# Row maxima split before they are turned: identity products in place of transposes, and a shorter VectorE list

## What is computed

```python
x = x + jnp.tanh(g_xattn[0]) * _L0_xattn_ref(_layernorm(x, axis=-1), ctx_1024, ...)
x = x + jnp.tanh(g_ffn[0]) * _L0_ffn_ref(_layernorm(x, axis=-1), ...)
# ... the same for layers 1, 2 and 3, each with its own attention and its own FFN
```

```python
attn = jnp.einsum('bhnd,bhmd->bhnm', q * scaling, k)
attn = jax.nn.softmax(attn, axis=-1)
out = jnp.einsum('bhnm,bhmd->bhnd', attn, v)
```

## Time and profile before

| | us |
|---|---|
| median of 3 runs | 1301.12 |
| lowest and highest of the 3 | 1295.35 and 1309.11 |
| span of the profiled execution | 1295.3 |
| TensorE busy in that span | 978.6 (76%) |
| VectorE busy | 778.0 (60%) |
| ScalarE busy | 570.7 (44%) |
| GpSimd busy | 391.1 (30%) |

### The profile page before, as it was taken

One profiled execution on the slowest core, in us unless ns is written; L12 is line 12 of the kernel. 1 busy time (PEld: TensorE's weight loads), 2 busy tenths in 40 slices (PEclk: granted clock), 3 DMA queues, 4 the chain that ended last, 5 costly groups with the idle time before them and its releaser, 6 DMA issues. The chain is left out here.

```text
span 1295.3 us, 19254 instructions
## 1 busy us (share of the span) xinstructions
PE 978.6 (76%) x5366; PEld 728.4 (56%) x5366; DVE 778.0 (60%) x1924; ACT 570.7 (44%) x1101; POOL 391.1 (30%) x519
## 2 busy tenths in 40 slices
PE   3788475688888988488888889478867578883765
PEld 2566353565565655256666666356755347773554
DVE  3687565576676667356666656447665424444665
ACT  1566242365455555245555554246643233321553
POOL 2432002122223213235555556423310132210212
PEclk9899576777677668689999999779987789996878
DMA  4000000000000000000000000100000100000001
GB/s 116 1 1 1 1 1 19 1 18 17 18 17 17 11 5 17 1 0 1 1 1 0 0 1 1 35 1 1 1 18 1 50 15 1 0 0 1 1 0 33
DMA packets 25577, 13.74 MB, mean 11 GB/s; under 512 B 10775, under 2 KB 25006, under 8 KB 25390
## 3 DMA queue, kind: packets, MB, share of 16 engines
q1 hardware_dynamic: 25518, 13.03, 3.7%
HBM read 11.98 MB, written 1.05 MB: 10 GB/s over the span
## 5 line engine op out<-in xcount | busy, mean ns | idle before, releaser
L1473 POOL TENSOR_TENSOR L1f_h<-L1f_h,L1f_gb 128x512 f32<-128x512 f32 (+1 forms) x96 | 151.6, 1581 | 120.0 <-DVE L1f_h L1763 99.5
L719 ACT ACTIVATE L_pt<-bank 128x512 f32<-128x512 f32 x224 | 131.0, 597 | 62.7 <-PE bank L605 59.6
L706 ACT ACTIVATE L_part<-bank,L_bias_ca,const 128x256 fp32r<-128x256 f32 x128 | 68.7, 562 | 118.7 <-PE bank L546 118.7
L407 POOL TENSOR_TENSOR L_kc<-L_kc_all,const 128x256 fp32r<-128x256 f32 x96 | 58.8, 616 | 186.3 <-PE bank L605 130.8
L1763 DVE TENSOR_TENSOR L1f_h<-L1f_a,bank 128x512 f32<-128x512 f32 (+1 forms) x96 | 65.5, 682 | 70.7 <-ACT L1f_a L1603 69.8
L1603 ACT ACTIVATE L1f_a<-bank 128x512 f32<-128x512 f32 (+1 forms) x96 | 57.2, 596 | 114.2 <-PE bank L1528 114.1
L1771 DVE TENSOR_TENSOR L1f_h_lo<-L1f_h,L1f_h_hi 128x512 fp32r<-128x512 f32 (+1 forms) x96 | 88.7, 925 | 11.3 <-ACT L1f_h_hi L1616 11.3
L845 DVE TENSOR_REDUCE L_ms<-bank 128x2 f32<-128x512 f32 x128 | 84.4, 687 | 16.1 <-PE bank L567 15.5
L567 PE MATMUL bank<-L_k,L_q 32*128 32x256 f32 x256 | 74.1, 402 | 11.9 <-DVE L_ms L845 8.9
L831 DVE SCALAR_TENSOR_TENSOR L_q<-bank,L_bias_c,L_part 128x256 fp32r<-128x256 f32 x96 | 46.3, 482 | 60.6 <-ACT L_part L706 56.0
L843 DVE TENSOR_REDUCE L_mc<-bank 128x8 f32<-128x512 f32 (+1 forms) x96 | 65.6, 683 | 22.8 <-PE bank L560 14.2
(11 more groups left out here) (405 smaller groups left out, 2613.4 us busy)
## 6 DMA issues: line engine op xcount, KB each, us to landing
L_raw<-in_L_ffn_w_dram SPq DMA_DIRECT2D x8, 176.0 KB, 2.3
L_raw<-in_L_ffn_v_dram SPq DMA_DIRECT2D x8, 176.0 KB, 2.4
const<-in_const_dram SPq DMA_DIRECT2D x1, 1036.0 KB, 4.9
x<-in_x_dram SPq DMA_DIRECT2D x2, 512.0 KB
L_raw<-in_L_ffn_w_dram SPq DMA_DIRECT2D x8, 128.0 KB, 2.4
L_mask<-in_mask_Bx1xSxS_ff_dram SPq DMA_DIRECT2D x2, 512.0 KB
out_dram<-x SPq DMA_DIRECT2D x2, 512.0 KB
L_raw<-in_L_ffn_w_dram SPq DMA_DIRECT2D x8, 48.0 KB, 2.5
```

The lines of the kernel that those rows point to most:

```text
L706: last = act.activation(part[:, i].bitcast(F32R), b_proj[:, i * S:(i + 1) * S], ACT.Identity, bias=bias_ca[:, i, g:g + 1], scale=pr.c("ak" ...
L719: act.activation(pt[:, g // 2, (g % 2) * NS + i], b_st[(g * NS + i) % 2][:], ACT.Exp, scale=scale).then_inc(sem["exp_done"], 1)
L1473: pool.tensor_tensor(h[0:m, r], h[0:m, r], gb[0:m, gate_slot(c)], ALU.mult).then_inc(sem["h_done"], 1)
```

## The change

Five edits, made in `attention` and, but for the second, in `attention3`.

1. VectorE no longer writes each maximum twice. It writes it once into the first row (`high`), and since `mx` is now fp32r the write rounds it. It then waits for its own write (`m_hi`) and writes what the rounding left into the second row (`low`). In layer 1 the maximum of `mc` and `ms` is also written whole into `m_all` beforehand, for that subtraction.
2. In layer 1 TensorE adds q into the same bank by a second product with the identity.
3. The two fp32 transposes of a group become ordinary products of fp32r operands with an fp32r copy of the identity, `ident_r`, which VectorE makes once in each layer's preparation.
4. ScalarE copies the bank into `mt` and raises `m_split` itself; it now waits until TensorE has used the older `mt`. The factors, `hm` and `hq` are gone.
5. VectorE's step `maxima` is gone, and with it the additions of 256 columns (L866, L868, L1247).

The core of the diff; `attention3` has the same edits but for `m_all` and q, and the rest are counts of the preparation and types.

```diff
-                        last = pe.transpose(b_mt[:, t * P:(t + 1) * P], mx[:, g % 2, t].rearrange("p j c -> p (j c)"), pr.id())
+                        ts = slice(t * P, (t + 1) * P)
+                        last = pe.matmul(b_mt[:, ts], mx[:, g % 2, t].rearrange("p j c -> p (j c)"), ident_r[:], start=True, stop=not gated)
+                        if gated:
+                            last = pe.matmul(b_mt[:, ts], ident_r[:], q[:, g, ts], start=False, stop=True)
                     last.then_inc(sem["m_turned"], 1)
...
                 def maxima(b, g):
                     act.wait_ge(sem["m_turned"], b * NG + g + 1)
-                    need(act, sem["m_split"], b * NG + g)
-                    act.activation(hm[:].bitcast(F32R), b_mt[:, 0:S], ACT.Copy, scale=pr.c("am1" if gated else "am")).then_inc(sem["m_hi"], 1)
+                    need(act, sem["st_done"], b * U + (g - 1) * NS)
+                    act.copy(mt[:, g % 2], b_mt[:, 0:S]).then_inc(sem["m_split"], 1)
...
+                prep(dve.tensor_copy(ident_r[:], pr.id()))
...
-                    dst = mx[:, g % 2].rearrange("p t j c -> p (t j) c")[:, :, at_row:at_row + 2]
-                    mcb = mc[:].rearrange("p t j -> p (t j)").unsqueeze(2).to_broadcast([P, 2 * GH, 2])
+                    high, low = (mx[:, g % 2, :, :, at_row + e] for e in range(2))
                     if own_keys:
-                        msb = ms[:].rearrange("p t j -> p (t j)").unsqueeze(2).to_broadcast([P, 2 * GH, 2])
-                        dve.tensor_tensor(dst, mcb, msb, ALU.max).then_inc(sem["m_ready"], 1)
+                        dve.tensor_tensor(m_all[:], mc[:], ms[:], ALU.max)
+                        dve.tensor_tensor(high, mc[:], ms[:], ALU.max).then_inc(sem["m_hi"], 1)
                     else:
-                        dve.tensor_copy(dst, mcb).then_inc(sem["m_ready"], 1)
-
-                def maxima(b, g):
+                        dve.tensor_copy(high, mc[:]).then_inc(sem["m_hi"], 1)
                     dve.wait_ge(sem["m_hi"], b * NG + g + 1)
-                    need(dve, sem["st_done"], b * U + (g - 1) * NS)
-                    if gated:
-
-                        need(dve, sem["m_split"], b * NG + g)
-                        dve.wait_ge(sem["qk_split"], b * NG + (g + 1))
-                        dve.tensor_tensor(hq[:], hm[:], q[:, g].bitcast(F32), ALU.add).then_inc(sem["hq_ready"], 1)
-                        dve.wait_ge(sem["hq_ready"], b * NG + (g + 1))
-                    dve.tensor_tensor(mt[:, g % 2], b_mt[:, 0:S], hq[:] if gated else hm[:], ALU.add).then_inc(sem["m_split"], 1)
+                    dve.tensor_tensor(low, m_all[:] if own_keys else mc[:], high.bitcast(F32), ALU.subtract).then_inc(sem["m_ready"], 1)
```

More of the change, by code:

```diff
@@ L209, in attention @@
         mc = sb("mc", [P, 2, GH])
-        mx = sb("mx", [P, 2, 2, GH, 32])
-        hm = sb("hm", [P, S])
+        mx = sb("mx", [P, 2, 2, GH, 32], F32R)
+        m_all = sb("m_all", [P, 2, GH])
+        ident_r = sb("ident_r", [P, P], F32R)
         mt = sb("mt", [P, 2, S], F32R)
@@ L251, in attention @@
         mask_a = sb("mask_a", [P, 1])
-        DVE_WEIGHTS = 10 if biased else 9
+        DVE_WEIGHTS = 11 if biased else 10
         DVE_READY = DVE_WEIGHTS + 4 + (2 if gated else 1) + (2 if masked else 0)
@@ L485, in _ @@
                 if biased:
-                    pe.wait_ge(sem["prep_dve"], 3)
+                    pe.wait_ge(sem["prep_dve"], 4)
                     for i in range(2):
@@ L903, in y @@
                     dve.scalar_tensor_tensor(xb, b_turn[:, 0:S].rearrange("p (t d) -> p t d", t=2), tg, xb, ALU.mult, ALU.add).then_inc(sem["x_done"], 1)
-                passes(dve, {"scale": scale_x, "turn": turn, "mask": mask, "proj": proj, "scores": scores, "maxima": maxima,
+                passes(dve, {"scale": scale_x, "turn": turn, "mask": mask, "proj": proj, "scores": scores,
                              "o_norm": o_norm, "o_scale": o_scale, "y": y})
@@ L940, in attention3 @@
         mc = sb("mc", [P, 2, H3])
-        mx = sb("mx", [P, 2, H3, 16])
-        hm = sb("hm", [P, S])
+        mx = sb("mx", [P, 2, H3, 16], F32R)
+        ident_r = sb("ident_r", [P, P], F32R)
         mt = sb("mt", [P, S], F32R)
@@ L1070, in _ @@
                 pe.wait_ge(sem["prep_act"], 12)
-                pe.wait_ge(sem["prep_dve"], 4)
+                pe.wait_ge(sem["prep_dve"], 5)
                 pe.wait_ge(sem["prep_pool"], 4)
@@ L1107, in maxima @@
                     for t in range(2):
-                        last = pe.transpose(b_mt[:, t * P:(t + 1) * P], mx[:, t].rearrange("p j c -> p (j c)"), pr.id())
+                        last = pe.matmul(b_mt[:, t * P:(t + 1) * P], mx[:, t].rearrange("p j c -> p (j c)"), ident_r[:], start=True, stop=True)
                     last.then_inc(sem["m_turned"], 1)
@@ L1184, in maxima @@
                     act.wait_ge(sem["m_turned"], b + 1)
-                    need(act, sem["m_split"], b)
-                    act.activation(hm[:].bitcast(F32R), b_mt[:, 0:S], ACT.Copy, scale=pr.c("a16")).then_inc(sem["m_hi"], 1)
+                    need(act, sem["st_done"], b * 2)
+                    act.copy(mt[:], b_mt[:, 0:S]).then_inc(sem["m_split"], 1)
                 def weights(b, h):
@@ L1216, in _ @@
                 dve.tensor_copy(self_[:].rearrange("p c n -> p (c n)"), pr.c("self3")).then_inc(sem["prep_dve"], 1)
+                dve.tensor_copy(ident_r[:], pr.id()).then_inc(sem["prep_dve"], 1)
                 dve.wait_ge(sem["prep_act"], 12)
@@ L1240, in scores @@
                     need(dve, sem["m_turned"], b)
-                    dve.tensor_copy(mx[:].rearrange("p t j c -> p (t j) c")[:, :, 0:2],
-                                    mc[:].rearrange("p t j -> p (t j)").unsqueeze(2).to_broadcast([P, 2 * H3, 2])).then_inc(sem["m_ready"], 1)
-                def maxima(b):
+                    dve.tensor_copy(mx[:, :, :, 0], mc[:]).then_inc(sem["m_hi"], 1)
                     dve.wait_ge(sem["m_hi"], b + 1)
-                    need(dve, sem["st_done"], b * 2)
-                    dve.tensor_tensor(mt[:], b_mt[:, 0:S], hm[:], ALU.add).then_inc(sem["m_split"], 1)
+                    dve.tensor_tensor(mx[:, :, :, 1], mc[:], mx[:, :, :, 0].bitcast(F32), ALU.subtract).then_inc(sem["m_ready"], 1)
                 def sums(b):
@@ L1270, in y @@
                     dve.scalar_tensor_tensor(xb, b_turn[:, 0:S].rearrange("p (t d) -> p t d", t=2), tg, xb, ALU.mult, ALU.add).then_inc(sem["x_done"], 1)
-                passes(dve, {"scale": scale_x, "turn": turn, "scores": scores, "maxima": maxima, "sums": sums, "parts": parts, "divide": divide, "y": y})
+                passes(dve, {"scale": scale_x, "turn": turn, "scores": scores, "sums": sums, "parts": parts, "divide": divide, "y": y})
 def ffn(pr, layer):
```

5 lines of the change are left out of this document (2 added, 3 removed).

## The result

| | before | after |
|---|---|---|
| median, us | 1300.79 | 1327.82 |
| lowest and highest | 1295.35, 1309.11 | 1317.45, 1329.29 |
| span of the profiled execution | 1295.3 | 1327.5 |

The ratio is 1.0177, with a 95% interval from 1.0122 to 1.0232: slower, by 27 us in the medians and 32 in the profiled executions. The forecast was 1323, with 1284 to 1338 as range. The number was met; most of its working was not, and the rest of this document is about that.

The account below looks back on a forecast made before the run. No engine is full: layers 0, 2 and 3 are rings of waits, layer 1 alternates between VectorE and TensorE. Layers 0 to 3 add +2.8, +12.5, +4 and +2.8, sum +22.1 us on 1295.3; against the median 1323, range 1284 to 1338.

Parts of the forecast that it names:

- cheap products: Rival on TensorE's new products: 0.11 us each, as fp32r or by the skill's table; total 1300, no change; chance 0.22.
- the new instruction has neither: TensorE: the product has neither transpose mode nor 256 columns, to which the low price belongs, so 0.22 us each.
- The lower bound of 0.10: TensorE: router logits with eight moving columns take 0.10 us each, so a full weight load is hardly cheaper than a transpose.
- dear products: Main case: each new TensorE product takes 0.22 us, +0.22 a group in layers 0, 2, 3, more in layer 1; chance 0.50.
- In the two at the lower clock TensorE pays 2 x 1.3: Layer 1: two of four groups a sequence run at the lower clock, each paying +1.3 us for four products.
- the clock in a rival: Rival on layer 1: relieved VectorE lets TensorE run without gaps, clock rises to 0.80, total 1286; chance 0.16.
- the hop: Layer 2: `m_split` comes from ScalarE, so some 0.55 of the mask's transposes' 0.67 us wait for L868 goes.
- 0 from the list: Layer 2: the gain from `m_split` is taken back, half by `low`, the rest by two other q writes; net 0.
- -0.8 on the list: Layer 0's q writes: two gain 0.1 us, one loses 0.2 to `low`, one gains 0.09; -0.1 a sequence.
- The place matters more: VectorE: `low` stands ahead of the q write, the wide addition stood behind it; `low` itself taken at 0.22 us.
- "collisions" rival: `m_all`, `high`, `low` stretched beside GpSimd, +0.39 us each: +12 in layer 1, some +4 elsewhere; total 1317; chance 0.12.
- VectorE's and ScalarE's terms: VectorE's small operations add 10 to 15 us busy time in layer 1; ScalarE's copy falls from 468 to 375 ns.

Follow-up runs that it names:

- the ninth experiment: Changed kernel with layer 1 put back as before the change, except that its two transposes are fp32r products; median 1326.45 us, ratio 1.0209 to the kernel before.
- The third experiment: Changed kernel with plain fp32 operands for the product that turns layer 1's maxima; median 1316.58 us, ratio 1.0104 to the kernel before.
- experiment 5: Changed kernel with layer 1 as before the change and `low` behind the q write in layers 0 and 2; median 1298.58 us, ratio 0.9923.
- 1: Changed kernel with layer 1 exactly as before the change; median 1302.22 us, ratio 1.0008 to the kernel before.
- 10: Changed kernel, but in layer 1 VectorE adds q and writes `mt`, and fp32 transposes turn the maxima; median 1297.6 us, ratio 0.9894 to the kernel before.
- 11: Layers 1 and 3 as before the change, layers 0 and 2 changed with `low` behind the q write; median 1291.49 us, ratio 0.9952.
- 12: Layer 1 of 10, layers 0 and 2 changed with `low` behind the q write, layer 3 as before the change; median 1288.8 us, ratio 0.9894.
- 2: Changed kernel, but in layer 1 VectorE adds q and writes `mt`, without TensorE's product with q; median 1316.75 us, ratio 1.0125 to the kernel before.

## Why the prediction was right, and where it was not

By its own last line the forecast was wrong in kind: it named two signs, cheap products and a clock of layer 1 that moves by over 0.05, and both came (0.05 us, and 0.60 for 0.71). That the number was met is luck.

**The price of the products: wrong.** The step was "the new instruction has neither, and is nearest to L661 in shape and four-byte operands. I take 0.22". It takes 0.05 at the upper clock as the second of a pair, and in layer 1's row of four up to 0.11 at the upper and 0.21 at the lower clock. The lower bound of 0.10 was wrong for a pair: I took it from the router logits, but those rows are plain fp32 records. For the row of four it came true. The chance of 0.50 rested on this one choice between two rows. By the Trainium skill's table ("VectorE: DVE Perf Modes", The TRN2 errata) a product of 128 columns takes, as an estimate, about 0.06 us. The pair's 0.05 agrees with it, the row of four doesn't, and I had set it aside with L661's 0.22, which only says that plain fp32 costs more.

**Layer 1, the number near, the mechanism missed.** I had +12.5 us from dear products at an unchanged clock (by its own terms, 1.6 x 8, it should read 12.8), and it was +29.5 us with cheap products at a lower clock. The step that failed is in the sum, "In the two at the lower clock TensorE pays 2 x 1.3": the number of groups at the lower clock was taken as given. I had the clock in a rival, but with the other sign: VectorE relieved, TensorE without gaps, clock up. What the runs showed in its place is that TensorE's own instruction in this spot carries the level: with products for transposes 80% of the time is at the lower level for 58%, and by the ninth experiment that alone costs 20 to 32 us. The third experiment has half of my dear case, two of a group's four products, and in its trace layer 1 is 17.6 us faster than in the cheap one. So the forecast of 1323 was met by a wrong price, which happened to stand for a loss of clock; the case that had the price right, "cheap products", gave 1300 and was off by 28 us.

**Layer 2: the sign was wrong, the hop was right.** Forecast 0 from the list and +4 from dear products; measured -4.5, of which some -3.0 at equal clock. The mask's transposes got `m_split` one hop sooner as described (0.67 us to at most 0.2). With the products at a quarter of the assumed price the +4 goes. I had the hop's gain of 0.55 us a sequence eaten up by `low`; with `low` behind the q write the layer gains 0.6 a sequence, and `low` at its place takes 0.2 of it back.

**Layer 0: +4.1 for +2.8, of which the wrong part was to be the larger.** I put -0.8 on the list and +3.6 on the products. With cheap products only the list is left, and it costs, some +1.7 at equal clock; the rest of the 4.1 lies in the first sequences, which ran at another clock, and no term had that. `low` ahead of the q write is worth some 3 us (experiment 5); it was stretched to 0.54 and 0.64 us in two of four groups of the later sequences. The place was named, "The place matters more"; its price was taken at 0.22, and the "collisions" rival had 0.39 more for one group in four.

**Layer 3: +2.0 for +2.8.** At equal clock it is 0.1 us a sequence, some +0.8: the wait for `mx` grew from 0.54 to 0.76, the 0.22 forecast, less ScalarE's 0.09, and the 0.22 for dear products wasn't there. The rest of the 2.0 lies in sequences of unequal clock.

**VectorE's and ScalarE's terms** held: 13.1 us added in layer 1 for 10 to 15, ScalarE's copy at 365 ns for 375. The figure of 0.26 us that the forecast worked out from the Trainium skill's 58 cycles (same page and section) was misapplied, since the page gives them for operands in SBUF and L868 reads a bank of PSUM; the sum didn't use it.

## What to carry to other kernels

Where the granted clock of a stage is between its levels, the clock is a term of the sum and not a constant: ask of each instruction taken from TensorE what level will be granted once it is gone, and price a change at both levels for the whole stage. A cheaper TensorE instruction can cost time (0.33 for 0.38 us a pair, and 20 to 32 us in layer 1), so take apart the TensorE part and the others of such a change and time each alone. A small operation put ahead of the one that others wait for can cost more than a wide one behind it (0.3 to 0.4 us a sequence in layer 0, 0.2 in layer 2). And compare stretches of equal clock before stage totals: with the same code a layer's total moved by 2 us and more, and five of its sequences at the full clock by 0.1 or less in layers 2 and 3 (0.9 in layer 0).

## What the runs showed of the hardware that I had not expected

- An fp32r product of 128 columns takes 0.05 us at the upper clock as the second of a pair, where an fp32 transpose of the same size takes 0.10. In a row of four, in which the maxima and the identity take turns as weights, the starts lie 0.11, 0.21 and 0.21 us apart at the lower clock, so from the third on a product there costs what a transpose does.
- With two transposes in each group layer 1 ran at mean clocks of 0.66 to 0.75 over six kernels (before, 1, 5, 10, 11, 12), with fp32r products in their place and no padding at 0.60 or 0.61 in three (after, 2, 9). Plain fp32 products gave 0.71.
- Two useless products of 512 columns a group made layer 1 of the changed kernel 19 us shorter at one place, and left it as long as it was at another.
- The kernel before spread from 1292.6 to 1310 us over all its runs. By and large the longer time went with the lower mean clock of the core, 0.851 at 1292.6 and 0.829 at 1306.3, though not in every run (1298.1 at 0.851, 1295.9 at 0.842).
- A GpSimd instruction beside it made VectorE's subtraction of 8 elements last 0.54 and 0.64 us for 0.17 to 0.18; each time it ended 0.02 to 0.04 us after GpSimd's.
